# Engine orders laid anew, TensorE fillers in the banks of the next step, and POOL spacers that nothing waits for

## The chip, the cores and the metric

One core of one Trainium2 chip runs the kernel. The metric is the device time in microseconds (us) of an execution. The profile is of one execution; its span runs from the first to the last instruction.

## The reference

`x` has 2 batches of 512 tokens of width 128. Four residual steps change it, each with a layer norm ahead of it:

```python
x = x + xcond(layernorm(x), ctx, ctx, tau, delta, L0 weights)   # cross attention, 16 heads of 8, 77 keys
x = x + ffn(layernorm(x), L0 weights)      # 8 experts as low-rank additions to one 128-512-128 network, relu
x = x + xcond(layernorm(x), ctx, ctx, tau, delta, L1 weights)
x = x + moe(layernorm(x), L1 weights)      # 8 experts w1 (128x512), w2 (512x128), gelu; top-1 routing,
                                           # result times the largest softmax probability of the router
```

The attention is softmax((q k^T tau + delta) / sqrt(8)) v per head, with biases on q, k, v and the output.

## The kernel before

Each engine runs a list of steps written out by hand (`TABLES`, one string for each of `pe`, `act`, `dve`, `pool`); `schedule()` expands it. `max/1/0/4:7` means the steps max/1/0/4, max/1/0/5 and max/1/0/6. The first two numbers are, in most steps, the layer l and the batch b, or the stage (0: attention 0, 1: ffn 0, 2: attention 1, 3: experts) and the batch. Each engine does its steps strictly in its order; semaphores tie the engines together.

The steps that matter here:
- `ln` and `xn`: layer norm. DVE takes the statistics (L714, L717), ACT the root (L596, L599), DVE makes XN (L732). For stage 3 of batch 1 POOL takes the root instead, as a power (L525).
- `xt`: TensorE transposes XN (L938), ACT copies it to XNT (L603). `q`: projection (L971), two instructions' worth of TensorE work for two head groups; ACT writes the high part (L629), DVE the low part (L770).
- `kp`, `ks`, `km`, `vp`: keys and values; masked keys KG are made on DVE for the first batch (L756) and on POOL for the others (L538). SP then places the values by small DMAs (L428).
- `max`: 16 per layer and batch. TensorE makes the scores of a head group and a query tile (L989), DVE takes the maxima (L780). `mt` transposes them (L998) back into QG. `sc`: transposed scores (L1014), then exp on ACT (L644). `pv`: the product with the values (L1029). `rd`: reciprocal denominators on ACT (L651, L654), `on`: normalised output OT on DVE (L790). `wo`: output projection (L1036), added to x on DVE (L799).
- `gate`, `ut`, `hid`, `out`: the ffn. `gate` has a chain of six short DVE operations and three products (L810 to L828) whose result `ut` transposes (L1057), `hid` multiplies (L1062, L1066), `out` adds up (L1076).
- `route` and `rank`: the router of the experts and the slot of each token; `row`: POOL scatters four tiles of rows of a batch to `slots` in DRAM, sorted by expert, by indirect DMA (L556). SP loads the sorted rows back in four pieces (L456). `m1/t`: TensorE transposes sorted tile t+1 (L1112), after waiting for its piece, and makes the hidden layer of tile t (L1119); ACT does gelu (L690); `m2`: second product (L1131), added up on DVE (L905, signal `z_ready`). `pb`: POOL makes bias times probability of a tile (L517), `bs` adds it on DVE (L900). `so`: POOL sends a finished tile to the output by indirect DMA (L566). There are 11 tiles per batch, 22 in all. `gap`: a spacer, a memset of XN on POOL (L559).

The results of TensorE that other engines read go through four PSUM banks (`shared`), which `banks()` hands out in turn over the steps of TensorE's order: `kp` takes two, each of max, q, xt, vp, mt, wo, gate, ut, hid, out, route and rank one. Ahead of a step `hold(key)` waits for the reader of the step that had the bank last, four such steps earlier. Where it stands differs: `q` waits for XNT, and `max` (where a new group begins) for the low part of q, and then calls `hold`; xt, mt, wo, ut, route and rank call `hold` first and wait for their input afterwards. `keep_busy(n, bank)` issues n bf16 matmuls of 512 columns whose result nobody reads. Nine open the kernel; the `busy` steps, in acc, stand elsewhere.

`finish(ins, signal)` on POOL lets an instruction signal and waits for that signal at once.

Of the kernel before, what the change touches and what calls it, by code (L numbers as in the profile page):

```python
# [1233 lines left out]
```

## Time and profile before

| | |
|---|---|
| median of three runs | 199.19 us (198.74 to 200.07) |
| the profiled execution | 199.31 us |
| its span | 197.5 us |
| TensorE busy (matmuls) | 164.6 us, 83% |
| DVE busy | 122.7 us, 62% |
| ACT busy | 98.1 us, 50% |
| POOL busy | 79.7 us, 40% |
| mean granted TensorE clock | 0.918 of 2.4 GHz |

The profiled execution's own time is 1.8 us over its span. Matmuls overlap, so that the busy time of TensorE is not its work at its peak. The slices of the page cut the span into 40 parts of 4.94 us. "idle before" in a row is the time in which the engine did nothing ahead of it, and behind the arrow stands what ended that; "issue" is where the trace shows nothing that was waited for.

### The profile page before, as it was taken

How to read it: one execution, taken by the hardware profiler on the slowest of the kernel's cores; microseconds unless marked ns; L12 is line 12 of the kernel's file. 1: busy time of each engine (PE TensorE's matmuls, PEld its weight loads, DVE VectorE, ACT ScalarE, POOL GpSimd, SP SyncE). 2: the span in 40 equal slices, each digit the busy share in tenths (PEclk: the TensorE clock that was granted, in tenths of full speed). 3: DMA queues.
4: the chain of work that ended last, by engine and by line, in shares of the span. 5: the costliest groups of instructions: out<-in, count | busy, mean ns of one | idle time of the engine just before them, and what ended most of it. 6: DMA issues, size and time to landing. Idle time of an engine off the chain costs nothing. (4 is left out here: it accounts for less than half of the span.)

```text
span 197.5 us, 3411 instructions
## 1 busy us (share of the span) xinstructions
PE 164.6 (83%) x879; PEld 117.9 (60%) x879; DVE 122.7 (62%) x359; ACT 98.1 (50%) x230; POOL 79.7 (40%) x110
## 2 busy tenths in 40 slices
PE   7678999999998587999998999908899769999500
...
PEclk9999999999999655599999999975999999999965
...
GB/s 184 160 2 3 6 3 84 166 0 2 3 0 0 0 2 3 5 3 33 278 400 490 352 9 25 61 83 241 4 14 67 70 267 39 16 7 8 35 9 0
DMA packets 14483, 15.48 MB, mean 78 GB/s; under 512 B 6842, under 2 KB 11205, under 8 KB 14400
## 3 DMA queue, kind: packets, MB, share of 16 engines
...
q8 instruction: 8, 0.13, 0.3%
...
## 5 line engine op out<-in xcount | busy, mean ns | idle before, releaser
L1029 PE MATMUL acc<-P,VP 123*128 123x512 f32 (+1 forms) x80 | 39.3, 593 | 0.0
L690 ACT ACTIVATE HT<-scores,B 128x128 f32<-128x128 f32 x88 | 25.2, 371 | 14.0 <-PE scores L1119 11.1
L547 POOL TENSOR_TENSOR X<-X,ROWS 128x512 f32<-128x512 f32 x6 | 7.6, 1272 | 55.6 <-DVE XN L732 55.5
L780 DVE TENSOR_REDUCE MR<-shared 128x4 f32<-128x308 f32 x64 | 26.6, 470 | 3.9 <-PE shared L989 3.4
L644 ACT ACTIVATE P<-scores 123x512 f32<-123x512 f32 (+1 forms) x40 | 22.9, 595 | 12.3 <-PE scores L1014 11.6
L566 POOL DMA_INDIRECT out<-XS,token x22 | 22.5, 1021 | 12.2 <-POOL XN L559 7.2
L1131 PE MATMUL acc<-W,HT 128*128 x176 | 23.1, 278 | 2.3 <-ACT HT L690 2.3
L1119 PE MATMUL scores<-XST,HT 128*128 128x128 f32 x176 | 24.8, 288 | 0.0
L989 PE MATMUL shared<-KG,QG 98*128 98x308 f32 x64 | 22.5, 415 | 1.1 <-DVE QG L770 0.8
L1119 PEld LDWEIGHTS scores<-XST,HT 128*128 128x128 f32 x176 | 22.9, 203 | 0.0
L1131 PEld LDWEIGHTS acc<-W,HT 128*128 128x128 f32 x176 | 21.1, 192 | 2.9 <-issue 2.9
L1014 PE MATMUL scores<-QG,KG 102*123 102x512 f32 (+1 forms) x48 | 22.4, 520 | 0.0
L556 POOL DMA_INDIRECT slots<-ROW,slot x8 | 8.2, 1031 | 29.4 <-issue 24.7
L1029 PEld LDWEIGHTS acc<-P,VP 123*128 123x128 f32 (+1 forms) x80 | 14.2, 190 | 7.4 <-issue 6.1
L892 DVE COPY HT<-W 128x512 f32 x22 | 12.6, 571 | 8.1 <-issue 5.3
L989 PEld LDWEIGHTS shared<-KG,QG 98*128 98x128 f32 x64 | 12.4, 206 | 7.7 <-DVE QG L770 3.2
L629 ACT ACTIVATE QG<-shared,ATT 64x512 fp32r<-64x512 f32 x16 | 10.9, 684 | 11.9 <-PE shared L971 11.6
L770 DVE SCALAR_TENSOR_TENSOR QG<-shared,ATT,QG 32x512 fp32r<-32x512 f32 x16 | 11.9, 745 | 5.4 <-ACT QG L629 5.0
L1112 PE MATMUL shared<-CON,XS 128*128 128x128 f32 x22 | 6.9, 312 | 8.4 <-DMA XS<-slots 8.3
L1014 PEld LDWEIGHTS scores<-QG,KG 102*123 102x123 f32 (+1 forms) x48 | 8.6, 185 | 8.1 <-issue 4.8
L924 PE MATMUL acc<-idle 128*128 128x512 bf16 x39 | 11.4, 427 | 1.6 <-DVE idle L705 1.5
L905 DVE SCALAR_TENSOR_TENSOR XS<-acc,XS 128x128 f32<-128x128 f32 x22 | 7.4, 344 | 8.4 <-PE acc L1131 8.0
...
## 6 DMA issues: line engine op xcount, KB each, us to landing
...
```

The source lines that it names most:

```text
L566: pool.indirect_dma_start(out, bass.IndirectOffsetOnAxis(ap=token[:, t:t + 1], axis=0), XS[:, t, 0:D], None, bounds_check=B * S - 1, oob_i ...
L644: act.activation(P[0:w, n % NP], scores[n % 2][0:w, :], ACT.Exp).then_inc(probs_ready, 1)
L690: ins = act.activation(HG1[:, t % NHB, c], hidden[t % 2][:, c], ACT.Gelu_apprx_tanh, bias=B1[:, bass.ds(expert[t] * NF + k, 1)])
L770: dve.scalar_tensor_tensor(QG[64:96, b, g], bank(s)[64 * odd:64 * odd + 32, :], ATT[l][0:32, A_BQ + g:A_BQ + g + 1], QG[0:32, b, g].bitcas ...
L780: dve.tensor_reduce(MR[:, b, qt, g, 2:2 + HG], bank(s)[:, 0:GK].rearrange("p (h k) -> p h k", h=HG), AX.X, ALU.max).then_inc(max_read, 1)
L892: dve.tensor_copy(W1C[:, n % NWC], W1[:, bass.ds(e * F, F)]).then_inc(w1_ready, 1)
L924: pe.matmul(unread[:, :], idle[:, 0:128], idle[:, 0:S], start=True, stop=True)
L989: pe.matmul(bank(s)[:, 0:GK], QG[0:ONES + 2, b, g, 128 * qt:128 * qt + 128], KG[0:ONES + 2, b, g, off:off + GK], start=True, stop=True).th ...
L1014: ins = pe.matmul(scores[n % 2][0:w, :], KG[:, b, g, c:c + w], QG[:, b, g], start=(i == 0), stop=(i == len(parts) - 1))
L1029: pe.matmul(acc[half][:, :], VP[0:w, l, b, j, half], P[0:w, n % NP, :], start=(j == 0), stop=(j == NT - 1)).then_inc(probs_used, 1)
L1119: ins = pe.matmul(hidden[t % 2][:, 128 * k:128 * (k + 1)], W1C[:, t % NWC, 128 * k:128 * (k + 1)], XST[:, t % 2], start=True, stop=True)
L1131: ins = pe.matmul(acc[n % 2][:, 0:D], HG1[:, n % NHB, 128 * k:128 * (k + 1)], W2[:, bass.ds(expert[n] * (NF * D) + D * k, D)], start=(k == ...
```

## The change

- New orders for all four engines. TensorE's `busy` steps are gone.
- `FILL` gives 14 steps a number of fillers, 58 in all (30 before, beside the first nine). `hold` issues them after its own wait, into the bank that the step is about to take.
- A `gap` no longer waits for its own memset, but ahead of it for that of the gap before.
- On POOL the root `ln/3/1` stands ahead of `pb/0` instead of behind it. `pb/8:10` and `pb/10` stand around so/1, and so/5 to so/18 are mixed anew with pb/11 to pb/21. 15 gaps remain.

The orders of TensorE and POOL are whole here; those of ACT and DVE are cut to their first lines.

```diff
     "pe": """
-        kp/0 xt/0/0 vp/0 busy/0/5 q/0/0/0:2 busy/0/5 max/0/0/0:3 busy/0/5 max/0/0/3:5 busy/0/1 max/0/0/5 busy/0/1
-        max/0/0/6 busy/0/1 max/0/0/7 busy/0/4 mt/0/0/0 max/0/0/8 xt/0/1 max/0/0/9:11 sc/0/0/0:2 max/0/0/11:13
-        q/0/1/0 sc/0/0/2:4 max/0/0/13:15 pv/0/0/0:2 max/0/0/15 max/0/1/0 sc/0/0/4 pv/0/0/2 mt/0/0/1 max/0/1/1:3
-        pv/0/0/3 max/0/1/3 sc/0/0/5 max/0/1/4 pv/0/0/4 sc/0/0/6:8 max/0/1/5:7 q/0/1/1 pv/0/0/5 max/0/1/7 sc/0/0/8
-        pv/0/0/6 mt/0/1/0 sc/0/0/9 max/0/1/8 pv/0/0/7:9 sc/0/1/0 max/0/1/9 pv/0/0/9 max/0/1/10:14 sc/0/1/1 pv/0/1/0
-        sc/0/1/2 max/0/1/14:16 sc/0/1/3 wo/0/0 sc/0/1/4 mt/0/1/1 pv/0/1/1:5 sc/0/1/5 xt/1/0 kp/1 gate/0 sc/0/1/6
-        pv/0/1/5 sc/0/1/7 pv/0/1/6 sc/0/1/8 ut/0 sc/0/1/9 pv/0/1/7 hid/0/0:4 pv/0/1/8:10 out/0 wo/0/1 xt/2/0 vp/1
-        q/1/0/0 xt/1/1 max/1/0/0:4 gate/1 max/1/0/4:7 ut/1 max/1/0/7 q/1/0/1 hid/1/0:3 max/1/0/8 mt/1/0/0 hid/1/3
-        sc/1/0/0:2 max/1/0/9:12 out/1 sc/1/0/2 max/1/0/12:14 pv/1/0/0 sc/1/0/3 max/1/0/14 pv/1/0/1 max/1/0/15
-        pv/1/0/2 sc/1/0/4 mt/1/0/1 pv/1/0/3 xt/2/1 pv/1/0/4 sc/1/0/5:7 q/1/1/0 sc/1/0/7 pv/1/0/5:7 max/1/1/0
-        sc/1/0/8 max/1/1/1:3 pv/1/0/7 max/1/1/3 sc/1/0/9 max/1/1/4:7 pv/1/0/8 max/1/1/7 pv/1/0/9 mt/1/1/0 q/1/1/1
-        wo/1/0 max/1/1/8 sc/1/1/0:2 max/1/1/9:12 pv/1/1/0 sc/1/1/2:4 pv/1/1/1 max/1/1/12 sc/1/1/4 xt/3/0
-        max/1/1/13:16 route/0 mt/1/1/1 pv/1/1/2:4 rank/0 sc/1/1/5 pv/1/1/4 sc/1/1/6 pv/1/1/5 sc/1/1/7:9 pv/1/1/6
-        sc/1/1/9 pv/1/1/7:10 busy/1/8 wo/1/1 m1/-1:2 xt/3/1 m2/0 route/1 m2/1 m1/2 rank/1 m1/3 m2/2 m1/4 m2/3 m1/5
-        m2/4 m1/6:8 m2/5 m1/8 m2/6 m1/9 m2/7 m1/10 m2/8 m1/11 m2/9 m1/12 m2/10 m1/13:15 m2/11 m1/15 m2/12:14 m1/16
-        m2/14 m1/17 m2/15:17 m1/18:20 m2/17 m1/20 m2/18:21 m1/21 m2/21
+        kp/0 vp/0 xt/0/0 q/0/0/0:2 max/0/0/0:8 mt/0/0/0 max/0/0/8 xt/0/1 max/0/0/9 sc/0/0/0:2 max/0/0/10:13 q/0/1/0
+        max/0/0/13 sc/0/0/2:4 max/0/0/14:16 pv/0/0/0:3 mt/0/0/1 max/0/1/0:3 sc/0/0/4 pv/0/0/3 max/0/1/3 sc/0/0/5
+        pv/0/0/4 sc/0/0/6:8 max/0/1/4:6 pv/0/0/5 max/0/1/6:8 q/0/1/1 pv/0/0/6 sc/0/0/8 mt/0/1/0 pv/0/0/7 max/0/1/8
+        sc/0/0/9 pv/0/0/8 max/0/1/9 sc/0/1/0 pv/0/0/9 max/0/1/10:12 sc/0/1/1 max/0/1/12 sc/0/1/2 max/0/1/13 pv/0/1/0
+        max/0/1/14:16 wo/0/0 sc/0/1/3:5 mt/0/1/1 pv/0/1/1:3 kp/1 sc/0/1/5:7 xt/1/0 pv/0/1/3 gate/0 pv/0/1/4 sc/0/1/7
+        pv/0/1/5:7 ut/0 sc/0/1/8 pv/0/1/7 hid/0/0:4 sc/0/1/9 pv/0/1/8 out/0 pv/0/1/9 vp/1 wo/0/1 xt/2/0 q/1/0/0
+        xt/1/1 max/1/0/0:4 gate/1 max/1/0/4:7 ut/1 max/1/0/7 q/1/0/1 hid/1/0:3 max/1/0/8 mt/1/0/0 hid/1/3 sc/1/0/0
+        max/1/0/9:11 sc/1/0/1 max/1/0/11 out/1 max/1/0/12 sc/1/0/2 max/1/0/13 pv/1/0/0:2 sc/1/0/3 max/1/0/14:16
+        pv/1/0/2 sc/1/0/4 xt/2/1 pv/1/0/3 mt/1/0/1 q/1/1/0 pv/1/0/4 sc/1/0/5:7 q/1/1/1 max/1/1/0:2 sc/1/0/7 pv/1/0/5
+        sc/1/0/8 max/1/1/2 pv/1/0/6 sc/1/0/9 max/1/1/3:7 pv/1/0/7 max/1/1/7 pv/1/0/8 max/1/1/8 pv/1/0/9 max/1/1/9:13
+        mt/1/1/0 max/1/1/13 wo/1/0 sc/1/1/0 max/1/1/14 sc/1/1/1 pv/1/1/0 sc/1/1/2:4 pv/1/1/1 max/1/1/15 xt/3/0
+        mt/1/1/1 route/0 pv/1/1/2 rank/0 sc/1/1/4 pv/1/1/3 sc/1/1/5:7 pv/1/1/4 sc/1/1/7 pv/1/1/5:7 sc/1/1/8:10
+        pv/1/1/7:10 wo/1/1 m1/-1:2 xt/3/1 m2/0 route/1 m2/1 m1/2 rank/1 m1/3 m2/2 m1/4 m2/3 m1/5:7 m2/4:6 m1/7 m2/6
+        m1/8:10 m2/7:9 m1/10 m2/9 m1/11 m2/10 m1/12:14 m2/11 m1/14 m2/12 m1/15 m2/13 m1/16:18 m2/14 m1/18 m2/15:18
+        m1/19 m2/18 m1/20 m2/19 m1/21 m2/20:22
     """,
     "act": """
-        ln/0/0 ks/0 xt/0/0 q/0/0/0 ln/0/1 q/0/0/1 mt/0/0/0 xt/0/1 sc/0/0/0:2 q/0/1/0 sc/0/0/2:4 mt/0/0/1 sc/0/0/4:8
+        ln/0/0 ks/0 xt/0/0 ln/0/1 q/0/0/0:2 mt/0/0/0 xt/0/1 sc/0/0/0:2 q/0/1/0 sc/0/0/2:4 mt/0/0/1 sc/0/0/4:8
...
     "dve": """
-        ln/0/0 xn/0/0 kp/0 ln/0/1 ks/0 vp/0 km/0/0 q/0/0/0:2 max/0/0/0:8 xn/0/1 mt/0/0/0 max/0/0/8:13 q/0/1/0
+        ln/0/0 xn/0/0 kp/0 ln/0/1 vp/0 ks/0 km/0/0 q/0/0/0:2 max/0/0/0:8 xn/0/1 mt/0/0/0 max/0/0/8:14 q/0/1/0
...
     "pool": """
         one/0 pre/0/0 km/0/1 pre/0/1 one/1 pre/1/0 km/1/0 pre/2/0 km/1/1 pre/1/1 pre/2/1 row/0/0 gap/0 row/0/1 gap/1
-        row/0/2 gap/2 row/0/3 pb/0 ln/3/1 pb/1:6 so/0 pb/6:8 so/1 pb/8:11 row/1/0 gap/3 row/1/1 gap/4 row/1/2 gap/5
-        row/1/3 gap/6 so/2 gap/7 so/3 gap/8 so/4 pb/11 so/5 pb/12 so/6 pb/13 so/7 pb/14 so/8 pb/15 so/9 pb/16 so/10
-        gap/9 so/11 pb/17 so/12 pb/18 so/13 gap/10 so/14 pb/19 so/15 pb/20 so/16 pb/21 so/17 gap/11 so/18 gap/12
+        row/0/2 gap/2 row/0/3 ln/3/1 pb/0:8 so/0 pb/8:10 so/1 pb/10 row/1/0 gap/3 row/1/1 gap/4 row/1/2 gap/5
+        row/1/3 gap/6 so/2 gap/7 so/3 gap/8 so/4 gap/9 so/5 pb/11 so/6 pb/12 so/7 pb/13 so/8 pb/14 so/9 pb/15 so/10
+        pb/16 so/11 gap/10 so/12 pb/17 so/13 pb/18 so/14 pb/19 so/15 pb/20 so/16 gap/11 so/17 gap/12 so/18 pb/21
         so/19 gap/13 so/20 gap/14 so/21
     """,
 }
+FILL = {('q', 0, 0, 0): 6, ('max', 0, 0, 0): 5, ('max', 0, 0, 3): 5, ('max', 0, 0, 4): 1, ('max', 0, 0, 5): 1, ('max',
+        0, 0, 6): 1, ('mt', 0, 0, 0): 5, ('wo', 0, 1): 7, ('q', 1, 0, 0): 3, ('xt', 1, 1): 5, ('max', 1, 0, 2): 1,
+        ('ut', 1): 7, ('wo', 1, 0): 2, ('wo', 1, 1): 9}
@@ -556,7 +558,9 @@
                     pool.indirect_dma_start(slots, bass.IndirectOffsetOnAxis(ap=slot[:, i:i + 1], axis=0), ROW[:, i], None,
                                             bounds_check=NS * 128 - 1, oob_is_err=False).then_inc(rows_sent[b], 16)
                 elif s[0] == "gap":
-                    finish(pool.memset(XN[:, 0, 0:3], 0.0), spaced)
+                    if s[1] > 0:
+                        pool.wait_ge(spaced, s[1])
+                    pool.memset(XN[:, 0, 0:3], 0.0).then_inc(spaced, 1)
                 elif s[0] == "pb":
                     bias_of(s[1])
                 elif s[0] == "so":
@@ -912,16 +916,17 @@
                 for signal, value in by if isinstance(by, list) else [by]:
                     pe.wait_ge(signal, value)
 
-            def hold(key):
-
-                if key in before:
-                    wait_reader(before[key])
-
             expert = {}
 
             def keep_busy(n, unread):
                 for _ in range(n):
                     pe.matmul(unread[:, :], idle[:, 0:128], idle[:, 0:S], start=True, stop=True)
+
+            def hold(key):
+
+                if key in before:
+                    wait_reader(before[key])
+                keep_busy(FILL.get(key, 0), bank(key))
 
             pe.wait_ge(idle_ready, 1)
             keep_busy(WARM, acc[1])
@@ -949,11 +954,6 @@
                                         ATT[l][:, A_K + QR * g:A_K + QR * (g + 1)], CTX[:, :, :], start=True, stop=True)
                         if g % 2 == 1:
                             ins.then_inc(full[use[key][0]], 1)
-                elif kind == "busy":
-                    _, late, n = s
-                    if late:
-                        pe.wait_ge(on_ready, 2 * 2 * B - 1)
-                    keep_busy(n, acc[1 - late])
                 elif kind == "vp":
                     l = s[1]
                     pe.wait_ge(in_att[l], 16)
```

In the cut part of DVE's order, `out/0 ln/2/0` now stand ahead of `on/0/1/1` (before, behind it), `vp/1` follows `ln/2/0`, and `bs/0:3` stand ahead of `m2/0`. ACT's `rd/0/0/0` and `rd/1/0/0:2` moved by a few steps.

## Rows read from the trace of the kernel before

**Rows 1.** Slices of the page: TensorE's busy tenths and its granted clock.
```profile
PE   7678999999998587999998999908899769999500
...
PEclk9999999999999655599999999975999999999965
```

**Rows 2.** Timeline, 176 to 197.5 us: start us, us, engine, line, work, idle before.
```profile
179.81 0.41 POOL L517 TENSOR_TENSOR PB<-B,XS 128x128 f32<-128x128 f32 x1
...
180.39 1.01 POOL L566 DMA_INDIRECT out<-XS,token  x1 [0.17 <-issue]
...
184.65 0.44 POOL L559 MEMSET XN<- 128x384 f32 x1
...
185.88 0.97 POOL L566 DMA_INDIRECT out<-XS,token  x1 [0.79 <-POOL XN L559]
...
186.84 0.35 DVE L905 SCALAR_TENSOR_TENSOR XS<-acc,XS 128x128 f32<-128x128 f32 x1 [2.81 <-PE acc L1131]
...
192.48 0.97 POOL L566 DMA_INDIRECT out<-XS,token  x1 [0.79 <-POOL XN L559]
```

**Rows 3.** Groups of POOL, 146 to 194 us: busy, mean ns, idle before.
```profile
L566 POOL DMA_INDIRECT out<-XS,token x20 | 20.4, 1020 | 9.0 <-POOL XN L559 7.2 <-issue 1.3 <-DVE XS L905 0.3
...
L559 POOL MEMSET XN<- 128x384 f32 x12 | 6.1, 506 | 0.0
...
L517 POOL TENSOR_TENSOR PB<-B,XS 128x128 f32<-128x128 f32 x11 | 4.8, 441 | 0.3
...
L556 POOL DMA_INDIRECT slots<-ROW,slot x4 | 4.1, 1027 | 3.2 <-POOL XN L559 1.6 <-issue 0.9 <-DVE XS L905 0.8
```

**Rows 4.** Timeline of POOL, 118 us to the end.
```profile
121.37 1.22 POOL L556 DMA_INDIRECT slots<-ROW,slot  x1 [23.80 <-issue]
...
146.43 1.04 POOL L556 DMA_INDIRECT slots<-ROW,slot  x1 [0.88 <-issue]
```

**Rows 5.** Waits: total us, times, longest.
```profile
DVE ROW L732 <- POOL rstd L525: 5.2, 1, 5.2
```

**Rows 6.** Timeline between the attention and the experts, 127 to 160 us.
```profile
127.11 1.13 PE L1036 MATMUL shared<-ATT,OT 128*128 128x128 f32 x8
...
130.39 0.17 DVE L720 TENSOR_SCALAR var_eps<-mean_var 128x4 f32<-128x4 f32 x1
...
133.25 0.48 PE L1112 MATMUL shared<-CON,XS 128*128 128x128 f32 x1 [5.01 <-DMA XS<-slots]
...
134.52 1.92 PE L1119 MATMUL scores<-XST,HT 128*128 128x128 f32 x8
...
134.59 1.05 POOL L525 TENSOR_TENSOR rstd<-var_eps,mhalf 128x4 f32<-128x4 f32 x1
...
137.90 0.60 PE L938 MATMUL shared<-CON,ROW 128*128 128x128 f32 x4
...
159.65 0.33 PE L1112 MATMUL shared<-CON,XS 128*128 128x128 f32 x1 [2.80 <-DMA XS<-slots]
```

**Rows 7.** Groups of TensorE, 66 to 83 us, then 20 to 62 us.
```profile
L971 PE MATMUL shared<-XNT,ATT 128*128 128x512 f32 x4 | 4.0, 1093 | 0.0
...
L971 PE MATMUL shared<-XNT,ATT 128*128 128x512 f32 x4 | 2.0, 594 | 0.0
```

**Rows 8.** Timeline of TensorE: a filler run, and three waits' surroundings.
```profile
8.75 1.24 PE L924 MATMUL acc<-idle 128*128 128x512 bf16 x5
...
62.22 1.06 PE L1036 MATMUL shared<-ATT,OT 128*128 128x128 f32 x8
...
66.46 1.09 PE L938 MATMUL shared<-CON,XN 128*128 128x128 f32 x4 [3.19 <-DVE XN L732]
...
108.06 1.13 PE L1036 MATMUL shared<-ATT,OT 128*128 128x128 f32 x8 [0.86 <-DVE OT L790]
```

**Rows 9.** Windows: us, busy PE, PEld, DVE, ACT, POOL, granted clock, DMA.
```profile
10.00:15.00 5.00, 3.65 (x12) 1.53 (x12) 4.84 (x9) 3.63 (x7) 4.63 (x7) 1.00 0.03 2
...
65.00:85.00 20.00, 16.51 (x46) 10.45 (x47) 15.07 (x42) 5.07 (x10) 4.97 (x4) 0.57 0.04 2
```

More of the change, by code:

```diff
@@ L87 @@
+        m1/19 m2/18 m1/20 m2/19 m1/21 m2/20:22
     """,
     "act": """
-        ln/0/0 ks/0 xt/0/0 q/0/0/0 ln/0/1 q/0/0/1 mt/0/0/0 xt/0/1 sc/0/0/0:2 q/0/1/0 sc/0/0/2:4 mt/0/0/1 sc/0/0/4:8
-        q/0/1/1 sc/0/0/8 rd/0/0/0 mt/0/1/0 sc/0/0/9 sc/0/1/0 rd/0/0/1 sc/0/1/1:4 mt/0/1/1 sc/0/1/4 ln/1/0 xt/1/0
-        sc/0/1/5 kp/1 sc/0/1/6 ks/1 sc/0/1/7:9 rd/0/1/0 hid/0/0 sc/0/1/9 hid/0/2 rd/0/1/1 ln/2/0 xt/2/0 ln/1/1
-        q/1/0/0 xt/1/1 q/1/0/1 hid/1/0 hid/1/2 mt/1/0/0 sc/1/0/0:4 ln/2/1 sc/1/0/4 mt/1/0/1 xt/2/1 sc/1/0/5:7
@@ L93 @@
-        q/1/1/0 sc/1/0/7 rd/1/0/0 sc/1/0/8:10 rd/1/0/1 q/1/1/1 mt/1/1/0 sc/1/1/0:2 ln/3/0 sc/1/1/2:4 xt/3/0 mt/1/1/1
-        route/0 sc/1/1/4:10 rd/1/1/0:2 m1/-1:1 xt/3/1 m1/1 route/1 m1/2:22
+        ln/0/0 ks/0 xt/0/0 ln/0/1 q/0/0/0:2 mt/0/0/0 xt/0/1 sc/0/0/0:2 q/0/1/0 sc/0/0/2:4 mt/0/0/1 sc/0/0/4:8
+        rd/0/0/0 q/0/1/1 sc/0/0/8 mt/0/1/0 sc/0/0/9 sc/0/1/0 rd/0/0/1 sc/0/1/1:4 mt/0/1/1 ln/1/0 sc/0/1/4 xt/1/0
+        sc/0/1/5 kp/1 sc/0/1/6 ks/1 sc/0/1/7:9 hid/0/0 rd/0/1/0 hid/0/2 sc/0/1/9 rd/0/1/1 ln/2/0 xt/2/0 ln/1/1
@@ L95 @@
+        q/1/0/0 xt/1/1 q/1/0/1 hid/1/0 hid/1/2 mt/1/0/0 sc/1/0/0:3 ln/2/1 sc/1/0/3 xt/2/1 sc/1/0/4 mt/1/0/1 q/1/1/0
+        sc/1/0/5:7 q/1/1/1 sc/1/0/7:10 rd/1/0/0:2 mt/1/1/0 sc/1/1/0:2 ln/3/0 sc/1/1/2 xt/3/0 sc/1/1/3 route/0
+        mt/1/1/1 sc/1/1/4:8 rd/1/1/0 sc/1/1/8:10 rd/1/1/1 m1/-1:1 xt/3/1 m1/1 route/1 m1/2:22
     """,
     "dve": """
-        ln/0/0 xn/0/0 kp/0 ln/0/1 ks/0 vp/0 km/0/0 q/0/0/0:2 max/0/0/0:8 xn/0/1 mt/0/0/0 max/0/0/8:13 q/0/1/0
-        max/0/0/13:16 max/0/1/0 mt/0/0/1 max/0/1/1:8 q/0/1/1 max/0/1/8 mt/0/1/0 on/0/0/0 max/0/1/9:13 on/0/0/1
@@ L99 @@
-        max/0/1/13:16 wo/0/0 ln/1/0 mt/0/1/1 xn/1/0 gate/0 ut/0 hid/0/1 ks/1 on/0/1/0 hid/0/3 on/0/1/1 out/0 ln/2/0
-        wo/0/1 xn/2/0 ln/1/1 xn/1/1 vp/1 q/1/0/0 max/1/0/0:4 gate/1 max/1/0/4:7 ut/1 max/1/0/7 q/1/0/1 hid/1/1
-        max/1/0/8 mt/1/0/0 hid/1/3 max/1/0/9:12 out/1 max/1/0/12 ln/2/1 max/1/0/13:16 xn/2/1 mt/1/0/1 q/1/1/0
-        max/1/1/0:8 on/1/0/0 mt/1/1/0 on/1/0/1 q/1/1/1 wo/1/0 ln/3/0 max/1/1/8:10 xn/3/0 max/1/1/10:16 route/0
-        mt/1/1/1 rank/0 tiles/0 cw/0:2 on/1/1/0 cw/2 on/1/1/1 cw/3 wo/1/1 ln/3/1 xn/3/1 cw/4:6 bs/0 m2/0 bs/1:3
@@ L104 @@
-        route/1 m2/1 rank/1 cw/6 m2/2 cw/7 bs/3 cw/8 bs/4:7 cw/9 tiles/1 m2/3 bs/7 cw/10 bs/8 cw/11 m2/4:6 bs/9
-        cw/12:14 m2/6:8 bs/10:13 m2/8 cw/14 m2/9 cw/15:17 bs/13 m2/10 bs/14 cw/17:19 m2/11 cw/19 m2/12 bs/15 m2/13
-        bs/16 m2/14 cw/20 bs/17:19 cw/21 m2/15:19 bs/19:21 m2/19 bs/21 m2/20:22
+        ln/0/0 xn/0/0 kp/0 ln/0/1 vp/0 ks/0 km/0/0 q/0/0/0:2 max/0/0/0:8 xn/0/1 mt/0/0/0 max/0/0/8:14 q/0/1/0
+        max/0/0/14:16 mt/0/0/1 max/0/1/0:8 q/0/1/1 mt/0/1/0 on/0/0/0 max/0/1/8:13 on/0/0/1 max/0/1/13:16 wo/0/0
```

8 lines of the change are left out of this document (added).

## The prediction

> **What bounds the kernel now.** I read the page's slices first. TensorE is busy nearly everywhere (digits 9 in slices 5 to 12, 8 and 9 from 17 to 26), with three weak places: slice 14, after which its clock is at half (5 in slices 15 to 17), slice 27, and the end, where it does nothing in the last two [rows 1]. The chain that ended last and the timeline of the end explain the last place. DVE adds the last expert output at 186.84, and everything after that is POOL sending rows out: the last indirect DMA starts at 192.48, the span ends at 197.5. POOL was not waiting for data. Where the order puts a spacer between two stores, one store follows the other after 0.97 + 0.44 + 0.79 us, and the 0.79 is POOL's own: it waits for the memset to report, and only then prepares the next DMA. Where a bias product stands between them (179.81) the next store starts 0.17 us after it, and the step is 1.61 us instead of 2.20 [rows 2]. So from the first scatter of batch 1 (146.43) POOL goes through 24 indirect DMAs, 12 spacers and 11 products with little other waiting, and sets the end [rows 3, 4]. That block starts where it does because of the routing of batch 1, and so the question is what makes that late. Among the waits, DVE's normalisation of batch 1 stands out: it waits 5.2 us for the root on POOL [rows 5]. In the timeline, the variance is there at 130.56, but POOL has a bias product ahead of the root, which needs sorted rows that land only at about 133.2; the root runs at 134.59 and TensorE transposes at 137.90 [rows 6]. The attention ahead of all this is TensorE's, by the same slices of 9 [rows 1].
>
> **The change part by part.** The sum starts from the profiled execution's 199.31 us (span 197.5 and 1.8 outside it), which is 0.1 above the median of the runs, 199.19.
>
> *Spacers not waited for (POOL).* What the new spacer waits for is the memset before the last DMA, done a DMA ago. The sequencer can then prepare the next DMA while the memset runs, as it does across a bias product. The trace shows no unwaited memset. The lower bound is the bias product's 0.17 us of idle time, the upper bound the present 0.79 (nothing saved), and below that the idle time could only be 0. I take 0.17: a product is the same case, one POOL instruction without a wait between two indirect DMAs, and it also loads a register first. That is 0.62 per interval. From row/1/0 on there are 12 such intervals: 7.4 us (0 to 9.5). Memset and product are alike in length, 0.51 and 0.44 on average [rows 3]. Three more lie in batch 0's scatters, from 121.37 on [rows 4]: 1.9 us, used below.
>
> *Root ahead of bias products, and the first scatter.* From the output projection of batch 1 (127.11 to 128.24) to xt/3/1 at 137.90 there are now 9.66 us. Two chains lead there. By DVE and POOL: variance 2.3 after the projection, root 1.05, four normalised tiles 1.31, so 133.0 on the present time axis. By TensorE: its order has three transposes and the hidden products of two tiles before xt/3/1, and the first transpose waits until 133.25 for sorted rows [rows 6]. These come 1.9 earlier by the spacers and 0.9 earlier because the new order has one scores and one pv step fewer ahead of rank/0: 130.45. From there to xt/3/1 the trace has 4.65 us, in which the first eight products take 1.92 us [rows 6], at half clock (digit 5 in slice 28); at full clock q's matmul takes 594 ns for 1093 [rows 7]. With 2.8 us less idle ahead of it the clock may hold, and then it is about 3.5. xt/3/1 comes at 133.95 (clock held) or 135.1 (not). TensorE's chain is the later one, so the root itself is hidden from then on. I take 3.6 us gained (2.8 to 3.9). Without the move of the root the gain would be none, since the first product still waits for rows. All of batch 1's routing and POOL's block move with it.
>
> *Is the end still POOL's?* Batch 1's first rows are awaited by TensorE for 2.80 us, until 159.65 [rows 6]. Four spacers fewer in its way bring them 2.5 us sooner, and the new order has one more product set (m2/8, 0.9) ahead of that wait: the wait is gone, and 2.8 us of TensorE's end with it. The last m1 stands ahead of two m2, no longer of one: 0.9 more. So z of tile 21 would come 3.7 us earlier relative to the block, and POOL's last store 7.4: 186.84 + 0.35 - 3.7 = 183.5 against 192.48 - 7.4 = 185.1. POOL still ends last, but by 1.6 us only. For pb/21, which now stands behind so/18, and for stores that wait for their tile I add 0.5 (0 to 2).
>
> *Fillers and orders, start.* A filler costs 0.215 us (five in 1.24, of which the last lasts 0.38) [rows 8]. Formerly they stood before the waits. Now each stands behind the wait for its bank, and for q behind the wait for XNT too: q/0/0/0 starts 6 x 0.215 = 1.3 later. DVE, busy 4.84 of the 5 us from 10 to 15 [rows 9], hides most of it: the four low parts end about 0.35 later than now, and the fillers ahead of max/0/0/3, which now wait for q's reader first, add 0.3. I take 0.7 lost (0 to 1.8).
>
> *Middle.* out/0 moves ahead of pv/0/1/9 (0.43, a pv step's spacing): -0.4. After the projection at 62.22 TensorE waits 3.19 us for normalised rows [rows 8], and then works at half clock: granted 0.57 over 65 to 85, with 16.5 us of busy TensorE and 15.1 of DVE [rows 9]. The new order fills this with seven fillers before wo/0/1, and 3, 5, 1 and 7 after. Along the chain xt/2/0, q/1/0/0, xt/1/1, gate/1, ut/1, q/1/0/1, hid lie about 12 of the 16.5 us, and q's matmul shows what they take at full clock, 594 ns against 1093 [rows 7]: 5.5 us less. DVE's own work in between takes back some 2. The fillers take another: those of q/1/0/0 stand behind XNT (0.65), and ut/1's bank was last gate/1's, whose reader makes just what ut/1 waits for, so its seven stand wholly in the way, 1.5 us, of which DVE's three pending maxima hide half. I take 2.2 gained (bounds: 5, what DVE's 15.1 of 20 us leave, and a loss of 3, below). At wo/1/0 TensorE waits 0.86 us [rows 8]; the new order has more maxima ahead of it: -0.5 (0 to -1.2). The 9 late fillers (8 before) run while OT is made, 2.0 us against 2.2: nothing.
>
> *Sum.* 199.3 + 0.7 - 0.4 - 2.2 - 0.5 - 3.6 - 7.4 + 0.5 = 186.4; on the median's level **186.3 us**.
>
> **Rivals.**
> *A: the spacers cost what they did.* If an indirect DMA behind an unwaited memset starts no sooner, 7.4 us and the 1.9 of batch 0 (1.5 at xt/3/1) stay, and the 0.5 goes: 186.3 + 8.4 = 194.7 us. For it: someone waited for these memsets, and after each the idle time is about 0.79. Against: after products it is 0.17, with nothing waited for [rows 2].
> *B: the clock falls in the middle all the same.* Then fillers cost 0.43 each, ten of them on the chain: 4.3 less the hidden half of ut's, about 3, lost instead of 2.2 gained. 186.3 + 5.2 = 191.5 us. For it: TensorE still has small gaps after 62. Against: from 10 to 15 us it was busy 3.65 of 5 and kept the full clock [rows 9]; I expect over 4 of 5 here. The Trainium skill (TensorE: Matmul & The Clock Gate, "A second HAM failure mode: psum-queue depth-cycling") says that small pauses from cycling through banks can be enough to make the clock swing; by that rule this rival, 191.5, would be the case. The trace, with four banks in turn and full clock at 3.65 of 5, does not agree so far.
> *C: an order leaves TensorE idle in the attention.* The orders were laid for slower transfers; one misplaced step between 20 and 62 or 85 and 125 stalls the queue behind it, since TensorE takes its steps in turn. Price of one such wait: that of L1036 or L938, 0.9 to 3.2 us [rows 8]: about 189.
> *D, slower than before.* The wait is what keeps the indirect DMA short: behind a memset still running, its descriptors are written more slowly, since both use POOL. The nearest row is 1.22 us for one [rows 4] against 0.97 [rows 2], which is 0.25. It decides from where the 12 intervals lose more than the other edits gain (5.5 us): each would have to be 0.46 longer than now, 2.7 us. At 2.9 the time is 202 us. No row comes near that.
>
> **How the numbers follow.** Forecast 0.60 (own range 183.5 to 188.5), A 0.10, B 0.12, C 0.13, D 0.03, and 0.02 for something not thought of. The range runs from 182.5 (the middle's and the block's better ends) to 193: it takes in B and C, and leaves out A and D and the far ends, under 2 in 10. A measurement here tells about 1% from no change. Faster by over 1%: all but D, part of the unknown and the worst of C and B together, 0.94. Within 1%: 0.02. Slower: 0.04.
>
> **What would show it.** Spacer steps right: in the block the memsets' followers idle about 0.17 us, not 0.79, and the last store starts some 2 us or less after the last z. The root right: it starts within 0.5 us after the variance, and DVE's wait for it is near 1. The scatter right: TensorE's wait for batch 0's first rows is about 2.5 us instead of 5.0, and the wait at batch 1's first rows is nearly gone. The middle right: granted clock over 0.9 between 65 and 85, where it was 0.57, and the first scores of layer 1 about 2 us sooner. The start right: DVE's first eight maxima end about 0.7 later. Wrong if the followers idle 0.7 or more (A), if the clock is near 0.5 after 65 (B), if TensorE's waits between 20 and 62 sum to over 2 us (C), or if the span ends on TensorE or DVE instead of POOL, in which case the block was not the bound.

## The result and the profile after

The kernel after takes 190.44 us (median of 4 runs, 189.69 to 190.81). The kernel before takes 199.41 us beside it (198.74 to 200.07). The ratio is 0.9546, with a 95% interval of 0.9499 to 0.9592. The profiled execution took 190.18 us and its span is 188.3. The forecast was 186.3, with a range of 182.5 to 193.0. So the sign was right and the size was not: 9 us gained where 13 were forecast. 190.44 lies inside that range, and outside the narrower 183.5 to 188.5 that the forecast called its own. Medians here and below are over all runs of a kernel, while the ratios and their intervals leave out the slow ones (over 1.5% above the kernel's fastest), so a ratio need not be the quotient of two medians.

The page's slices, TensorE's tenths and its clock, as [rows 1] before:

```profile
PE   6668999999999987699999989895899999999940
...
PEclk9999999999999999699999999999579999999997
```

The half-clock stretch of slices 15 to 17 is down to one digit 6 in slice 17, and at the end TensorE does nothing in the last slice only, where it did nothing in two. Slices 24 and 26, in layer 1's attention, have an 8, where before had a 9 in each of slices 23 to 26. Slice 28 is the entry of the experts: TensorE's digit is a 5, where it was a 0 (slice 27). The clock still falls there (5 and 7 in slices 29 and 30).

The end, in the timeline, as [rows 2]:

```profile
181.15 0.43 POOL L563 MEMSET XN<- 128x384 f32 x1
181.75 0.97 POOL L570 DMA_INDIRECT out<-XS,token  x1 [0.17 <-issue]
181.81 0.35 DVE L909 SCALAR_TENSOR_TENSOR XS<-acc,XS 128x128 f32<-128x128 f32 x1 [1.28 <-PE acc L1131]
182.70 0.45 POOL L563 MEMSET XN<- 128x384 f32 x1
183.31 0.97 POOL L570 DMA_INDIRECT out<-XS,token  x1 [0.17 <-issue]
```

The step over a spacer is 183.31 - 181.75 = 1.56 us, where it was 2.20. The idle time behind a memset is the 0.17 that stands behind a bias product, no longer 0.79. The last store starts 1.15 us after the last z (what DVE adds up for the last tile, L909) has ended; before it was 5.29.

POOL's groups from 145 us to the end, as [rows 3], and the first scatter of batch 1:

```profile
L570 POOL DMA_INDIRECT out<-XS,token x20 | 20.2, 1009 | 3.4 <-issue 2.9 <-DVE XS L909 0.3 <-DMA XS<-slots 0.2
L563 POOL MEMSET XN<- 128x384 f32 x12 | 5.6, 464 | 0.0
L519 POOL TENSOR_TENSOR PB<-B,XS 128x128 f32<-128x128 f32 x11 | 4.8, 439 | 0.3
L558 POOL DMA_INDIRECT slots<-ROW,slot x4 | 4.0, 992 | 2.0 <-issue 2.0
```
```profile
145.63 1.05 POOL L558 DMA_INDIRECT slots<-ROW,slot  x1 [1.50 <-issue]
```

POOL's block is what it does from the first scatter of batch 1 (row/1/0) to the last store. Inside it (so without the idle time ahead of row/1/0) POOL idles 3.4 + 0.3 + 2.0 - 1.5 = 4.2 us, where it was 9.0 + 0.3 + 3.2 - 0.9 = 11.6. It is 183.31 - 145.63 = 37.68 us long, from start to start, before 46.05. It starts 0.80 sooner (146.43 before). 8.4 + 0.8 is the 9.2 us by which the last store is earlier.

The middle and its windows (us, then busy PE, PEld, DVE, ACT, POOL, clock, DMA), as [rows 9], and the same lines before:

```profile
74.74 0.67 PE L989 MATMUL shared<-KG,QG 98*128 98x308 f32 x3
77.04 0.61 PE L923 MATMUL shared<-idle 128*128 128x512 bf16 x1 [1.63 <-DVE U L832]
77.87 2.34 PE L923 MATMUL shared<-idle 128*128 128x512 bf16 x5 [0.22 <-DVE MR L784]
80.00 0.84 PE L1057 MATMUL shared<-CON,U 128*96 128x128 f32 x4
...
86.63 0.43 PE L1014 MATMUL scores<-QG,KG 102*123 102x512 f32 x1
```
```profile
65.00:70.00 5.00, 3.81 (x20) 2.18 (x19) 4.03 (x15) 1.31 (x5) 2.85 (x3) 1.00 0.06 3
70.00:75.00 5.00, 3.98 (x25) 2.58 (x23) 4.88 (x11) 1.97 (x3) 2.14 (x2) 1.00 0.07 4
75.00:80.00 5.00, 3.15 (x9) 1.24 (x10) 2.93 (x12) 0.00 (x0) 0.00 (x0) 0.71 0.07 4
...
65.00:85.00 20.00, 15.94 (x67) 8.92 (x67) 15.81 (x42) 5.33 (x11) 4.99 (x4) 0.91 0.07 4
```
```profile
77.51 1.06 PE L1057 MATMUL shared<-CON,U 128*96 128x128 f32 x4 [1.29 <-DVE U L828]
...
86.60 0.66 PE L1014 MATMUL scores<-QG,KG 102*123 102x512 f32 x2
```

The last fence is of the kernel before. The clock held until TensorE's wait that ends at 77.04, and over 65 to 85 it is 0.91, over the 0.9 that the forecast named as its sign, and yet the first scores of layer 1 (L1014) start at 86.63, where they started at 86.60. What ut/1 transposes (U) was there at 77.04. The fillers stand behind the wait for it, run at half clock (2.34 us for five, against 1.24 in [rows 8]) and hold ut/1 back to 80.00.

Between the attention and the experts, as [rows 6]:

```profile
128.57 1.16 PE L1036 MATMUL shared<-ATT,OT 128*128 128x128 f32 x8
...
131.70 0.47 PE L1112 MATMUL shared<-CON,XS 128*128 128x128 f32 x1 [1.97 <-DMA XS<-slots]
131.88 0.17 DVE L724 TENSOR_SCALAR var_eps<-mean_var 128x4 f32<-128x4 f32 x1
132.13 1.05 POOL L527 TENSOR_TENSOR rstd<-var_eps,mhalf 128x4 f32<-128x4 f32 x1 [4.05 <-DVE var_eps L724]
...
133.20 1.91 PE L1119 MATMUL scores<-XST,HT 128*128 128x128 f32 x8
...
135.12 1.91 PE L1119 MATMUL scores<-XST,HT 128*128 128x128 f32 x8
...
136.82 1.06 PE L943 MATMUL shared<-CON,ROW 128*128 128x128 f32 x4
```

The root follows the variance at once, and TensorE waits 1.97 us for the first sorted rows instead of 5.01. Its wait for batch 1's first rows, 2.80 us before, is gone: that transpose starts at 156.87 with no idle time ahead of it. From batch 0's first rows (131.70) the 5.12 us to xt/3/1 run at half clock: 1.91 us for eight products twice, where before the second eight took 1.62. In all xt/3/1 comes 8.25 us after the start of the output projection; before it was 10.79. And the projection itself starts 1.46 later.

### The profile page after: what moved, and what is told of

Read it like the earlier page. It is cut to its first block, busy times and chain, and to the rows that moved or that the text cites. A ratio compares the mean times of both kernels' runs of the same rounds, so it can differ in the third digit from the quotient of the medians.

```text
span 188.3 us, 3446 instructions
## 1 busy us (share of the span) xinstructions
PE 165.8 (88%) x902; PEld 117.3 (62%) x907; DVE 123.2 (65%) x359; ACT 97.7 (52%) x230; POOL 79.3 (42%) x110
## 4 chain that ended last, share of the span: by engine, by line
PE 62%; DVE 15%; POOL 6%; issue 5%; DMA 5%; ACT 3%; POOLq 1%; ACTq 0%; SPq 0%; DVEq 0%
PE acc L1029 14%; PE scores L1119 9%; PE acc L1131 7%; PE scores L1014 5%; PE shared L1076 4%; PE shared L1062 4%; PE shared L989 3%; DVE MR L784 3%; PE shared L971 3%; PE shared L923 3%; DVE QG L774 2%; DVE XN L736 2%; POOL out L570 2%; DMA X<-in_x 2%; PE shared L1036 2%
## 5 line engine op out<-in xcount | busy, mean ns | idle before, releaser
L1029 PE MATMUL acc<-P,VP 123*128 123x512 f32 (+1 forms) x80 | 39.8, 595 | 0.4 <-ACT P L648 0.4
L1131 PEld LDWEIGHTS acc<-W,HT 128*128 128x128 f32 x176 | 21.6, 195 | 1.6 <-issue 1.6
L989 PE MATMUL shared<-KG,QG 98*128 98x308 f32 x64 | 21.7, 408 | 0.1
L1014 PE MATMUL scores<-QG,KG 102*123 102x512 f32 (+1 forms) x48 | 21.4, 503 | 0.1
L923 PE MATMUL shared<-idle 128*128 128x512 bf16 x53 | 15.1, 408 | 6.5 <-ACT XNT L607 2.0
L896 DVE COPY HT<-W 128x512 f32 x22 | 11.9, 539 | 6.1 <-issue 5.6
L909 DVE SCALAR_TENSOR_TENSOR XS<-acc,XS 128x128 f32<-128x128 f32 x22 | 7.6, 346 | 12.4 <-PE acc L1131 12.2
L989 PEld LDWEIGHTS shared<-KG,QG 98*128 98x128 f32 x64 | 11.6, 190 | 6.1 <-issue 3.1
L923 PEld LDWEIGHTS shared<-idle 128*128 128x128 bf16 x58 | 5.4, 102 | 14.7 <-issue 6.1
L1014 PEld LDWEIGHTS scores<-QG,KG 102*123 102x123 f32 (+1 forms) x48 | 8.5, 185 | 7.3 <-issue 4.1
```

Of the source, the lines that this page charges most:

```text
L896: dve.tensor_copy(W1C[:, n % NWC], W1[:, bass.ds(e * F, F)]).then_inc(w1_ready, 1)
L923: pe.matmul(unread[:, :], idle[:, 0:128], idle[:, 0:S], start=True, stop=True)
L989: pe.matmul(bank(s)[:, 0:GK], QG[0:ONES + 2, b, g, 128 * qt:128 * qt + 128], KG[0:ONES + 2, b, g, off:off + GK], start=True, stop=True).th ...
L1014: ins = pe.matmul(scores[n % 2][0:w, :], KG[:, b, g, c:c + w], QG[:, b, g], start=(i == 0), stop=(i == len(parts) - 1))
L1029: pe.matmul(acc[half][:, :], VP[0:w, l, b, j, half], P[0:w, n % NP, :], start=(j == 0), stop=(j == NT - 1)).then_inc(probs_used, 1)
L1131: ins = pe.matmul(acc[n % 2][:, 0:D], HG1[:, n % NHB, 128 * k:128 * (k + 1)], W2[:, bass.ds(expert[n] * (NF * D) + D * k, D)], start=(k == ...
```

## The experiments

Each ratio is to the kernel before on the same chip, with its 95% interval. Times "in the trace" are of one execution of each.

**e1, e2, e3: the two POOL edits alone, on the kernel before.**

```diff
 e1, e3:
-                    finish(pool.memset(XN[:, 0, 0:3], 0.0), spaced)
+                    if s[1] > 0:
+                        pool.wait_ge(spaced, s[1])
+                    pool.memset(XN[:, 0, 0:3], 0.0).then_inc(spaced, 1)
 e2, e3:
-        row/0/2 gap/2 row/0/3 pb/0 ln/3/1 pb/1:6 so/0 ...
+        row/0/2 gap/2 row/0/3 ln/3/1 pb/0:6 so/0 ...
```

> The kernel before with one edit: spacers not waited for. Theory (the spacers are nearly all of the change): followers of a memset idle 0.17 us instead of 0.79; batch 0's last scatter 1.9 us sooner, POOL's block from row/1/0 to the last store 7.4 shorter (46.05 to about 38.6), 199.3 - 9.3 = 190 us, up to 191 if TensorE's last tile then comes last. Rival (orders, fillers and the root carry a third or more of the 9 us): 193 us or above.

> The kernel before with one edit: the root on POOL ahead of the first bias product. Theory (hidden behind TensorE's own first two tiles): the root starts within 0.5 us of the variance, 4 us sooner, xt/3/1 moves by under 0.3, the time by under 0.4 (199.0 to 199.4). Rival (DVE's 5.2 us wait for the root set xt/3/1): xt/3/1 and the time 2 to 4 us sooner, about 196.

> The kernel before with both POOL edits and neither the new orders nor the fillers. Theory (these two are the change, and the spacers bring rows soon enough for the root to matter): 189.5 to 190.5, level with the changed kernel or just under it, as the new orders end the attention 1.5 us later. Rival (the new orders pay): the changed kernel stays 1.5 us or more ahead, 192 or above here.

e1 took 189.98 us (0.9528, 0.9478 to 0.9578), as much as the whole change. In its trace the block is 183.74 - 145.30 = 38.44 us, batch 0's scatters take 5.29 from first to last for 7.21, and the first rows come at 131.29. e2 took 199.71 (1.002, 0.9988 to 1.0052): its root runs at 130.70, four us sooner, and xt/3/1 at 138.13 against 137.90. The root was hidden behind the wait for rows, as the prediction had it. e3 took 188.97 (0.9512, 0.9454 to 0.9569), which its interval doesn't tell from e1. From the output projection to xt/3/1 it takes 9.49 us in e3's trace and 9.37 in e1's, so the root stays hidden with the rows earlier too.

**e5: all the rest of the change,** that is, the kernel after with `finish` back and `pb/0` ahead of `ln/3/1` again.

> The changed kernel with both POOL edits taken back: spacers wait again, the root stands behind pb/0; orders and fillers as changed. Theory (orders and fillers are level with the old ones: the middle gains nothing, the attention of layer 1 ends 1.5 us later, one product set fewer stands behind batch 1's rows): 198.5 to 200.5 us. Rival (they are worth 2 us or more, as the prediction's middle had it): 197 or less.

199.82 us (0.9997, 0.9959 to 1.0036). With waited spacers the orders and fillers gain nothing. The last store in the timeline of e5:

```profile
190.98 0.44 POOL L561 MEMSET XN<- 128x384 f32 x1
192.22 0.97 POOL L568 DMA_INDIRECT out<-XS,token  x1 [0.79 <-POOL XN L561]
```

With the wait back the 0.79 is back, and the block sets the end as before. That hides what orders and fillers would do to TensorE, so e4, e6 and e7 look at them with free spacers.

**e4, e6, e7: the fillers, in the kernel after.** e4 drops `('ut', 1): 7`, e6 sets `FILL = {}` (the nine that open the kernel stay), and e7 has the seven ahead of the wait and, since their own bank isn't free yet there, in acc[1]:

```diff
-        ('ut', 1): 7, ('wo', 1, 0): 2, ('wo', 1, 1): 9}
+        ('wo', 1, 0): 2, ('wo', 1, 1): 9}
...
                 elif kind == "ut":
+                    if b == 1:
+                        keep_busy(7, acc[1])
                     hold(key)
```

> The changed kernel without the seven fillers ahead of ut/1. Theory (they stand behind the product that ut/1 waits for, and cost 3 us at half clock): ut/1's transposes start at about 77.1 instead of 80.0, the clock falls all the same around 77 since TensorE idles 1.9 us there and works slower behind it, so that the first scores of layer 1 come 1 to 2.5 us sooner and the time is 188 to 189.5. Rival (the fillers are what keeps the clock up after 78, or DVE bounds that stretch): within 0.5 of the changed kernel, or slower.

> The changed kernel with an empty table of fillers (the nine opening ones stay). Theory (the fillers pay with the clock between 65 and 77 what they cost at q and ut/1): 189.5 to 191.5, within 1 us of the changed kernel, clock near 0.5 from 66 on, and TensorE's clock less sure at the start. Rival (without them the clock falls at the start as well): 193 or more.

> The changed kernel with ut/1's seven fillers ahead of the wait for the bank, written to the accumulator that is free there. Theory (place, not number, was wrong): they fill the 1.9 us in which TensorE idled, the clock stays full from 62 to 85, ut/1's transposes start within 0.2 of the product, the first scores of layer 1 come 2.5 to 3 us sooner, the time is 187 to 188.5. Rival (DVE bounds that stretch, whatever TensorE's clock): 189.5 or more.

e4: 189.38 us (0.9498, 0.9447 to 0.9549), not told from after. In its trace ut/1 starts at 78.75 at half clock, and the first scores come 19.98 us after wo/0/1 (67.20), where after has 20.87. From ut/1 to the first scores it takes 8.43 us, where after has 6.63. So leaving the seven out gives only 0.9 of the 3 by which they hold ut/1 back: behind it they had brought the clock up again. The clock of e4 had fallen at about 76.0, before TensorE's wait and not behind it:

```profile
75.27 1.25 PE L1049 MATMUL shared<-W,XNT 128*128 128x40 f32 x8
76.33 1.12 PE L989 MATMUL shared<-KG,QG 98*128 98x308 f32 x3
```

The same three products take 0.67 us in after. TensorE had been busy without a break since 74.77, and none of its idle stretches since 60 was longer than 0.73 us.

e6: 190.65 us (0.9549, 0.9511 to 0.9587), not told from after, so the 58 fillers together are worth nothing that shows. In its trace the clock over 65 to 85 is 0.57 as before, and the middle takes 24.67 us, 0.7 more than in after. e7: 188.18 us (0.9401, 0.9346 to 0.9455). Its middle in the timeline, and its window:

```profile
76.36 1.69 PE L923 MATMUL acc<-idle 128*128 128x512 bf16 x7
78.23 0.61 PE L1059 MATMUL shared<-CON,U 128*96 128x128 f32 x4 [0.19 <-DVE U L832]
...
84.91 0.43 PE L1014 MATMUL scores<-QG,KG 102*123 102x512 f32 x1
```
```profile
65.00:85.00 20.00, 17.59 (x81) 9.88 (x80) 18.07 (x51) 7.68 (x15) 4.99 (x4) 1.00 0.07 4
```

The same seven now lie in TensorE's idle time, ut/1 follows U by nothing, and the clock is whole over the 20 us. From the end of the ffn (DVE's add of out/0, 63.78) to the first scores it takes 21.13 us, where after took 23.96 and before 24.11. The place was wrong, not the number. The gain shows in the times too: e7's interval lies below after's.

**e8: the old orders,** both POOL edits, and fillers in acc[1] in front of the waits: 14 before xt/2/0, 3 before xt/1/1, 7 before ut/1, 14 before the first sorted rows.

> Old orders with both POOL edits, and fillers only ahead of waits in which TensorE idles: 14 before xt/2/0, 3 before xt/1/1, 7 before ut/1, 14 before the first sorted rows, all into a free accumulator. Theory: clock full from 62 to 85 (2.5 to 3.5 us) and at the experts' first tiles (1 to 1.5 us): 184 to 186 us. Rival (DVE bounds the middle, DMA the experts' start): 188 or more, level with the run of both POOL edits.

188.44 us (0.9455, 0.9421 to 0.949): a miss, better than after but not the 184 to 186 hoped for. In the middle the clock still fell, at about 74.0, with TensorE busy for the 1 us ahead and 1.50 us idle up to 71.03, so that the seven fillers took 2.79 us; it took 21.9 us from out/0's add to the first scores. What held is the entry of the experts:

```profile
125.81 3.19 PE L926 MATMUL acc<-idle 128*128 128x512 bf16 x14
129.21 0.33 PE L1117 MATMUL shared<-CON,XS 128*128 128x128 f32 x1 [0.21 <-DMA XS<-slots]
...
132.44 0.60 PE L941 MATMUL shared<-CON,ROW 128*128 128x128 f32 x4
```

From the first rows to xt/3/1 it is 3.23 us, where after had 5.12. What the low clock costs there is 1.9 us, since the wait for the second piece of rows inside it is much the same (0.83 us in e8, 0.76 in after).

**e9, e10: fillers ahead of the waits, in the kernel after.** e9 moves those of q (8 and 3) in front of the wait for XNT; e10 does that, has e7's, and nine more ahead of the first sorted rows.

```diff
 e9, e10:
+                    if (b, pair) == (0, 0):
+                        keep_busy((8, 3)[l], acc[1])
 e10, in m1, ahead of the wait for the first sorted rows:
+                        keep_busy(9, acc[1])
```

> The changed kernel with the fillers of q/0/0/0 (eight now) and of q/1/0/0 (three) ahead of the wait for XNT, in a free accumulator. Theory (the 2 us in which TensorE idles before them is what lets the clock fall near 10 us in some executions, 1.1 to 1.4 us each time, and they delay q by 1.3): first eight maxima end at 19.6 instead of 20.05, no digit under 9 in the first slices, 189 to 190 us with less spread. Rival (start and clock there are chance): no difference from the changed kernel, 190.4.

> The changed kernel with the fillers of q and ut/1 ahead of their waits, and nine more ahead of the first sorted rows. Theory (places add up): q 0.5 to 1, ut/1 2.8, experts' first tiles 1 to 1.5 (first rows to xt/3/1 3.3 us instead of 5.1): 185 to 186.5 us, under every run so far. Rival (POOL's block takes nothing from an earlier xt/3/1, or DMA bounds the first tiles): 188.

e9: 189.2 us (0.9404, 0.9348 to 0.9459). Its single runs lie between 186.14 and 193.18, with a mean granted clock of 0.989 in the quickest and 0.951 in the slowest, so the hoped for smaller spread wasn't seen. Its median is 0.948 of the kernel before's, 199.57, which is hardly below after's interval, so that e9 can't be told clearly from after. What DVE does behind the first eight maxima starts at 19.54 for 20.05 in after, and out/0's add at 62.17 for 62.67; but the middle then takes 24.50 us for 23.96, with the clock at 0.90 from 70 to 75 and 0.50 from 75 to 80. e10: 187.07 us (185.48 to 188.91; ratio 0.9347, 0.9292 to 0.9401), the lowest median here. It is faster than after; from e7 and e9 its interval doesn't tell it. The profiled execution is its fastest, 185.48. Its clock by slice there, and its entry of the experts:

```profile
PE   6968999999999986999999989999889999899940
...
PEclk9999999999999999999999999999999999999996
```
```profile
126.21 2.10 PE L923 MATMUL acc<-idle 128*128 128x512 bf16 x9
128.47 0.33 PE L1117 MATMUL shared<-CON,XS 128*128 128x128 f32 x1 [0.16 <-DMA XS<-slots]
...
131.58 0.60 PE L943 MATMUL shared<-CON,ROW 128*128 128x128 f32 x4
```

Every slice of the clock but the last, in which TensorE has nothing left to do, is a 9. That is this execution: three of the other five have a mean granted clock of 0.968 to 0.971, where this one has 0.992. The middle takes 83.27 - 62.13 = 21.14 us, the entry 3.11, and the first scatter of batch 1 comes at 140.40. The last store starts at 178.62, 4.7 us ahead of after's; the medians are 3.4 us apart.

**e11, e12: without spacers.** e11 is the kernel before with all 15 gone; e12 is e1 without the six from row/1/0 to so/4.

> The kernel before with all 15 spacers taken out. Theory (a spacer does something for the next indirect DMA, which is why a product serves as well): back to back, an indirect DMA starts 0.6 us or more after the last one's end, or lasts over 1.5, so that nothing is won over spacers that aren't waited for, 190 us or above. Rival (the spacers are plain cost): indirect DMAs follow each other every 1.0 to 1.15 us, 12 x 0.5 less in POOL's block, which then is no longer the last; the last tile is, and the time is 188 to 189 us.

> The kernel of e1 (unwaited spacers, nothing else of the change) without the six spacers from row/1/0 to so/4, so that seven indirect DMAs of batch 1 follow each other with nothing of POOL between them; the nine other spacers stay. In e11, with no spacer at all, TensorE's experts reached batch 1 early and then the trace has a stretch, 145.4 to 148.7 us, in which ACT and DVE both wait for a TensorE result of 145.4, just while POOL starts an indirect DMA every 1.28 us; and after the last three stores back to back gelu waits 1.85 us from the start of its products where e1 has 1.20. Theory 1: a row of indirect DMAs back to back holds up what TensorE, ACT and DVE hand to each other, and this is what spacers are for. Then the stretch is there again between row/1/0 and so/4, 2 to 3 us of ACT and DVE idle on a TensorE result, the last z is 1 to 3 us later than e1's 181.75, and the time is 190.5 to 193, though POOL itself gets through the seven DMAs 2 us sooner. The end of the kernel, where the spacers stay, is as in e1. Theory 2: the stretch was of that one execution, or comes from elsewhere, and spacers only cost POOL their time. Then POOL gains 6 x 0.3 = 1.8 us or more there, is then ahead of DVE, and the last z sets the end: 188 to 189.5. If the time is as e1's 189.98 but the stretch is seen, the two cancel.

e11: 193.39 us (192.18 to 196.3; ratio 0.9669, 0.9613 to 0.9725), 3.4 us more than with unwaited spacers. Back to back an indirect DMA starts every 1.28 to 1.35 us, 0.97 to 1.04 long and with 0.30 of idle time, so the DMAs themselves are no slower. But in its timeline:

```profile
146.79 0.98 POOL L556 DMA_INDIRECT slots<-ROW,slot  x1 [0.30 <-issue]
...
148.69 1.14 ACT L690 ACTIVATE HT<-scores,B 128x128 f32<-128x128 f32 x4 [3.42 <-PE scores L1119]
148.70 0.60 DVE L892 COPY HT<-W 128x512 f32 x1 [3.31 <-PE scores L1119]
...
150.58 2.00 PE L1119 MATMUL scores<-XST,HT 128*128 128x128 f32 x8 [3.22 <-ACT XST L683]
...
151.16 0.97 POOL L566 DMA_INDIRECT out<-XS,token  x1 [2.12 <-DVE XS L905]
```

ACT and DVE stand still together, both on a TensorE result, just while the scatters follow each other; TensorE does nothing for 3.22 us and then works at half clock (2.00 us for eight products); the stores then wait for z, and the last z comes at 185.00. e12 was to tell whether the missing spacers do that. It took 189.09 us (0.9489, 0.9444 to 0.9534):

```profile
147.78 0.98 POOL L556 DMA_INDIRECT slots<-ROW,slot  x1 [0.30 <-issue]
149.07 0.97 POOL L556 DMA_INDIRECT slots<-ROW,slot  x1 [0.30 <-issue]
...
152.91 0.97 POOL L568 DMA_INDIRECT out<-XS,token  x1 [0.30 <-issue]
...
181.55 0.35 DVE L907 SCALAR_TENSOR_TENSOR XS<-acc,XS 128x128 f32<-128x128 f32 x1 [3.11 <-PE acc L1133]
...
182.69 0.97 POOL L568 DMA_INDIRECT out<-XS,token  x1 [0.78 <-DVE XS L907]
```

Seven DMAs back to back, and nothing stands still: TensorE is busy for 5.00 of 5 us from 145 to 150, as in e1. Theory 1 falls for this stretch. so/4 starts 2.8 us sooner than in e1 (155.69 there), and the last store only 1.05 (183.74), because the last store now waits for z. So once the spacers are not waited for, POOL has hardly more than a microsecond of its own at the end, and removing spacers buys little. Why e11 is slow stays open: its runs all lie above 192, the stretch is seen in its one trace, and the spacers of batch 0 and of the last stores, which it lacks and e12 has, were not taken out by themselves.

## Why the prediction was right in sign and short in size

*Spacers: right, and all of the gain.* The 12 intervals at 0.62 us each were to give 7.4, and the idle time inside the block fell by just that, 11.6 to 4.2. The block shrank by 8.4 (in e1 by 7.6), since memsets and DMAs were also 0.8 shorter, and the 0.5 that I had added for other waits didn't come. Batch 0's scatters gave 1.91 for the 1.9 named. The idle time behind the memset is exactly the 0.17 of the bias product, the nearest row that I went by. Rivals A and D are out.

*Root: right that it is hidden* (e2, e3), and right that it starts within 0.5 us of the variance: 132.13 after 131.88 and 0.17.

*First scatter: 2.5 for 3.6.* The rows came as early as said. The step that failed is "with 2.8 us less idle ahead of it the clock may hold". It did not, with 1.97 us idle ahead of the rows; e8 and e10 with 0.2 idle had it whole and took 3.1 to 3.2 us. For the clock not held I had named 135.1, which is 2.8 gained; it became 2.5, since the trace has 5.12 us there and not the 4.65 that I went by. So the sum's 3.6 needed fillers in front of the wait for rows, not only a shorter wait.

*Start: 0.5 for the 0.7 at the first maxima,* and of that 0.2 is left at out/0. e9, which has its fillers (eight for six) ahead of the wait for XNT, gets all of it back in its one trace.

*Middle: 2.2 forecast, 0.15 measured.* This is the term that failed. Split at U, after against before, from out/0's add: U comes 0.65 sooner, the fillers hold ut/1 for 2.96, and from ut/1 to the first scores it takes 6.63 us for 9.09, 2.46 less. In the forecast's own terms the clock's gain was 5.5, less DVE's 2, less 0.65 for q's fillers, so 2.85; the trace has 0.65 + 2.46 = 3.1. That is the size forecast, in part by luck: by e4, 1.8 us of the 2.46 are what ut/1's fillers gave back by bringing the clock up again, and the forecast had the clock never fall. What was mis-sized is ut/1's seven fillers: 0.75 on the chain (1.5 us, half hidden, at full clock), and they took 2.96. The text had them "wholly in the way", but not that TensorE, which idles 1.63 us there, loses its clock just before them, so that they run at half, nor that they would hide next to nothing. That is 2.2 us, all that the middle lacks. e7 confirms the reading: with the seven moved, 2.8 us come back.
That the sign named for this part, a clock over 0.9, came true without the 2 us is a warning: the clock of a stretch isn't the time of its chain. Rival B's own sign, a clock near 0.5 after 65, didn't come; its fillers at half clock did, for ut/1's.
The rule cited for rival B (the Trainium skill, "TensorE: Matmul & The Clock Gate", "A second HAM failure mode: psum-queue depth-cycling") is not settled here. In after, with four banks in turn and TensorE busy 3.81 and 3.98 of 5 us, the granted clock was 1.00, and it fell only at the end of an idle stretch of 1.63 us: that trace doesn't agree. In e4, which has the same steps up to there, it fell in mid-work behind idle stretches of at most 0.73 us, as the rule would have it. What makes the clock fall there in one execution and not in another stays open.

*wo/1/0: 0.5 gained forecast, 1.4 lost by wo/1/1.* The 0.86 us wait is gone, as said, but more steps stand ahead of wo/1/0, and it starts 1.2 us later, counted from layer 1's first scores. This is rival C, and the traces show it alone: from the first scores of layer 1 to wo/1/1 it takes 40.48 to 40.51 us in all seven traces with the old orders (86.60 to 127.11 before), and 41.94 or 41.95 in all six with the new ones and these fillers. In e6, with the new orders and no fillers, it is 42.10, so it isn't the fillers. The new orders cost 1.4 us there, whatever the clock did ahead. The windows of before and then of after:

```profile
110.00:115.00 5.00, 5.00 (x22) 2.97 (x20) 4.93 (x20) 3.09 (x7) 0.00 (x0) 1.00 0.65 247
115.00:120.00 5.00, 5.00 (x27) 3.08 (x28) 4.18 (x19) 2.15 (x5) 0.00 (x0) 1.00 0.00 0
```
```profile
110.00:115.00 5.00, 4.48 (x19) 2.56 (x18) 4.53 (x17) 2.19 (x5) 0.00 (x0) 1.00 0.01 3
115.00:120.00 5.00, 4.33 (x26) 2.43 (x24) 3.20 (x16) 2.50 (x5) 0.00 (x0) 1.00 0.00 0
```

TensorE was full there and now has 1.2 us of holes in ten. Which of the moved steps makes them wasn't tried; e8, with the old orders and fillers ahead of waits, takes 1.4 us less here than e10, and yet isn't faster; its trace has the low clock in the middle that e10's has not.

*The end: still POOL's, and close.* I had 1.6 us between the end of the last z and the last store, the trace has 1.15, and e12 shows that DVE's last z is now nearly as late: 2.8 us off POOL, 1.05 off the end.

*The sum again.* Forecast terms and what the traces show: start and out/0 +0.3 and +0.2; middle -2.2 and -0.15; attention with wo/1/0 -0.5 and +1.4; scatter -3.6 and -2.5; block -7.4 + 0.5 and -8.4. The forecast sums to -12.9, the measured terms to -9.45, and the last store moved by -9.17 (0.3 is lost between xt/3/1 and the first scatter).
